# A cross network over looked-up rows: six tables instead of eight by one-hot products, and transfers in another order and queue

## The reference

```python
def _cin_layer(h0, h, W):
    Wr = W.reshape(F0, Fi, K)
    return jnp.einsum('bid,bjd,ijk->bkd', h0, h, Wr)
conv1 = _cin_layer(x, x, W1)           # 39 x 39 pairs -> 128
hidden1, final1 = conv1[:, :64, :], conv1[:, 64:, :]
conv2 = _cin_layer(x, hidden1, W2)     # 39 x 64 pairs -> 128
z = jnp.sum(jnp.concatenate([final1, conv2], axis=1), axis=2)
h = jnp.concatenate([z, dense_ctx], axis=1)
h = jnp.maximum(h @ W_top1 + b_top1, 0.0)
h = jnp.maximum(h @ W_top2 + b_top2, 0.0)
y = h @ W_top3
```

## Time and profile before

| | |
|---|---|
| median of 3 runs | 844.24 us (842.39 to 844.51) |
| profiled execution, its own time | 845.87 us |
| its span in the trace | 844.1 us |
| mean granted TensorE clock | 0.97 of full |
| busy: TensorE, VectorE, ScalarE, GpSimd | 91%, 84%, 69%, 63% |
| DMA | 180.90 MB, mean 214 GB/s |

### The profile page before, as it was taken

How to read it: one execution, slowest core, us unless ns; L and a number is a source line. 1 busy time by engine, 2 the same in 40 slices (tenths; PEclk the granted TensorE clock), 3 DMA queues, 4 the chain that set the end, 5 groups by cost and what they waited for, 6 DMA issues and landing times.

```text
span 844.1 us, 16070 instructions
## 1 busy us (share of the span) xinstructions
PE 764.4 (91%) x5816; PEld 446.9 (53%) x5816; DVE 709.4 (84%) x1176; ACT 579.6 (69%) x1547; POOL 531.1 (63%) x508
## 2 busy tenths in 40 slices
PE   1996268789999999999999999999999999999996
PEld 0563113236556656564656555655656656666666
DVE  5994469769899999888989889898989899999850
ACT  1331225748878787877687878787888888787872
POOL 6887777747777777767676767777777777400000
PEclk9998589979999999999999999999999999999999
DMA  5444988898989898989888888889898989888200
GB/s 129 141 100 130 263 208 223 245 258 237 256 238 261 232 254 233 241 226 244 232 231 235 231 243 227 254 230 253 228 251 240 255 222 281 230 263 268 77 2 1
DMA packets 137125, 180.90 MB, mean 214 GB/s; under 512 B 106587, under 2 KB 117699, under 8 KB 119061
## 3 DMA queue, kind: packets, MB, share of 16 engines
q1 hardware_dynamic: 119444, 170.27, 70.8%
q0 software_dynamic: 16128, 8.29, 6.1%
q10 hardware_dynamic: 1472, 1.30, 0.5%
HBM read 167.57 MB, written 17.21 MB: 219 GB/s over the span
## 4 chain that ended last, share of the span: by engine, by line
PE 29%; DMA 28%; DVE 24%; SPq 11%; issue 4%; ACT 2%; POOL 1%; ACTq 0%; DVEq 0%
DMA copies<-xt 25%; DVE blocks L774 21%; PE hidden L430 13%; SPq L351 9%; PE sums L457 4%; PE sums L477 4%; PE hidden L532 3%; DVE turned L796 2%; PE sums L506 2%; POOL emb L396 1%; ACT arena L631 1%; PE sums L482 1%; DMA blocks<-hot_t 1%; PE sums L494 1%; PE sums L498 1%
## 5 line engine op out<-in xcount | busy, mean ns | idle before, releaser
L396 POOL DMA_INDIRECT emb<-in_tbl,ids_tile x504 | 530.9, 1053 | 199.3 <-issue 93.2
L774 DVE TENSOR_TENSOR blocks<-copies 117x512 f32<-117x512 f32 x840 | 522.5, 690 | 91.8 <-DMA copies<-xt 51.7
L430 PE MATMUL hidden<-blocks,w_pairs 117*64 117x512 f32 x1792 | 433.9, 610 | 26.0 <-DVE blocks L774 24.0
L631 ACT ACTIVATE arena<-sums 64x480 f32<-64x480 f32 (+2 forms) x936 | 293.7, 314 | 152.0 <-PE sums L457 130.6
L430 PEld LDWEIGHTS hidden<-blocks,w_pairs 117*64 117x64 f32 x1792 | 149.5, 138 | 235.4 <-DVE blocks L774 110.0
L457 PEld LDWEIGHTS sums<-xdiag,turned 64*103 64x103 f32 x2000 | 98.2, 167 | 78.3 <-issue 34.1
L619 ACT ACTIVATE xdiag<-turned 32x468 f32<-32x468 f32 (+1 forms) x256 | 118.8, 464 | 3.1
L457 PE MATMUL sums<-xdiag,turned 64*103 64x78 f32 x2000 | 112.2, 257 | 1.8
L602 ACT ACTIVATE hid_high<-hidden 32x512 f32<-32x512 f32 x128 | 75.3, 589 | 14.0 <-PE hidden L430 12.0
L477 PE MATMUL sums<-arena,weights 128*128 128x128 f32 x640 | 82.9, 287 | 1.9 <-DVE weights L851 1.3
L477 PEld LDWEIGHTS sums<-arena,weights 128*128 128x128 f32 x640 | 77.0, 199 | 4.4 <-DVE weights L851 1.5
(11 more groups left out here) (49 smaller groups left out, 311.1 us busy)
## 6 DMA issues: line engine op xcount, KB each, us to landing
copies<-xt SPq DMA_DIRECT2D x448, 312.0 KB
emb<-in_tbl,ids_tile POOLq DMA_INDIRECT x504
xt<-emb SPq DMA_DIRECT2D x32, 152.0 KB
xt<-xt SPq DMA_DIRECT2D x16, 304.0 KB
blocks<-hot_t SPq DMA_DIRECT2D x8, 500.0 KB
xt<-emb SPq DMA_DIRECT2D x32, 104.0 KB
hot_kept_rows<-rows SPq DMA_DIRECT2D x4, 480.0 KB, 9.0
emb<-hot_kept_rows SPq DMA_DIRECT2D x15, 128.0 KB
```

What stands on the lines that cost most here:

```text
L396: pool.indirect_dma_start(out=emb[u][:, f * D:(f + 1) * D], out_offset=None, in_=tables[f], in_offset=bass.IndirectOffsetOnAxis(ap=ids_til ...
L430: mm = nc.tensor.matmul(hidden[64 * c:64 * c + 64, k % 2, bank, :], w_pairs[0:ROWS, t, bank * HALF_HID:bank * HALF_HID + HID], blocks[0:RO ...
L631: op = nc.scalar.activation(out[:, :, cols].rearrange("p h (u b) -> p h u b", u=2), g[rows, i], ACT.Copy)
L774: op = nc.vector.tensor_tensor(blocks[0:ROWS, at + c, :], a[:, cols], b[:, cols], ALU.mult)
```

## The change

Six of the 1000-row tables are looked up by products (12 lookups), so tiles 1 to 15 have 33 gathers each. The split tables move from `weights` to the buffers of copies 2 and 3, and the layers' weights are loaded in `first_tile` behind the index loads. `keep` moves from SyncE's to ScalarE's queue. In the loads of chunk 1 nothing stands between the copies, and the load of the stored rows stands before them. All products with 128 output columns are made in two halves of 64. In the tail, VectorE takes over half of the last sort, the last tile's `final_sums` waits for ScalarE's copies only before its second part, and the copy of the dense rows comes first.

```diff
-HOT = [0, 4, 10, 13, 16, 26, 28, 29]
+HOT = [0, 4, 10, 13, 16, 26]
-TABLES = 5
+TABLES = 4
...
+        tables_at = copies[0:HOT_P, 2:4, :].rearrange("p a b -> p (a b)")
-        hot_table = [weights[0:HOT_P, n % TABLES * PART_WORDS:...
+        hot_table = [tables_at[:, n % TABLES * PART_WORDS:...
...
-        FIRST_SPILLED = [5, 7, 7]
-        AT_ONCE = 24
+        FIRST_SPILLED = [5, 5, 5]
+        AT_ONCE = 36
...
                 elif chunk == 1:
                     sp.wait_ge(hot_looked, COPIES_FREE)
+                elif v in (2, 3):
+                    sp.wait_ge(hot_looked, LOOKUPS)
...
                     index(n)
...
-                    if n % 2 and n >= 7:
-                        keep((n - 7) // 2)
+                    if n == 4:
+                        sp.dma_start(weights[:, 0:N_FIN], finals).then_inc(fin_loaded, 16)
+                    if n == 5:
+                        sp.dma_start(weights[:, N_FIN:], layers).then_inc(mlp_loaded, 16)
                     spill(0, 0, [s for s in range(len(PARTS)) if FIRST_SPILLED[s] == n])
                 sp.wait_ge(spilled[0], 16 * SPILLS)
                 for v in LOAD_ORDER:
                     load_copy(0, 0, 0, v)
-                keep(KEPT - 3)
-                load_copy(0, 0, 1, 0)
-                load_copy(0, 0, 1, 1)
-                keep(KEPT - 2)
-                load_copy(0, 0, 1, 2)
-                load_copy(0, 0, 1, 3)
-                keep(KEPT - 1)
                 load_hot_rows(1)
-                load_copy(0, 0, 1, 4)
+                for v in LOAD_ORDER:
+                    load_copy(0, 0, 1, v)
                 spill(0, 1)
...
             def final_sums(tile, u, j):
                 if j == 0:
-                    pe.wait_ge(gram_out, 2 * N_GROUPS * (tile + 1))
                     if tile == TILES - 1:
+                        pe.wait_ge(gram_out, N_GROUPS * (CHUNKS - 1))
                         pe.wait_ge(gram2_out, N_GROUPS + 1)
+                    else:
+                        pe.wait_ge(gram_out, 2 * N_GROUPS * (tile + 1))
...
+                    if n == FH and tile == TILES - 1:
+                        pe.wait_ge(gram_out, 2 * N_GROUPS * (tile + 1))
                     if n < FH:
-                        mm = nc.tensor.matmul(fin_conv2, w_fin2[:, n, :], gram2[:, n, cols],
-                                              start=(n == 0), stop=(n == FH - 1))
+                        for c in range(2):
+                            part = slice(64 * c, 64 * c + 64)
+                            mm = nc.tensor.matmul(fin_conv2[part, :], w_fin2[:, n, part], gram2[:, n, cols],
+                                                  start=(n == 0), stop=(n == FH - 1))
...
             def sort_hidden(k, chunk):
-                for bank in range(BANKS):
+                for bank in range(1 if chunk == CHUNKS - 1 else BANKS):
...
+            def keep(m):
+                act.wait_ge(hot_copied, 4 * (m + 1))
+                act.dma_start(hot_kept_rows[1:TILES, :, 2 * m * D:2 * (m + 1) * D].rearrange("t p n -> p t n"),
+                              rows[:, m % 2, 1:TILES].rearrange("p t a d -> p t (a d)")).then_inc(hot_kept[m % 2], 16)
...
             for j in range(LOOKUPS):
                 stage(j)
+                if j % 4 == 1 and j > 4:
+                    keep((j - 5) // 4)
...
             copy_rows(LOOKUPS - 1)
+            keep(KEPT - 1)
...
+            def sort_last(k, chunk):
+                dve.wait_ge(hid_turned, 2 * chunk - 1)
+                dve.wait_ge(hid_pairs, pairs_done(chunk, LAST, 1))
+                for q in (1, 3):
+                    op = nc.vector.tensor_copy(hid_high[32 * q:32 * q + 32, :], hidden[32 * q - 32:32 * q, k % 2, 1, :])
+                op.then_inc(last_sorted, 1)
...
+            def dense_copy(tile):
+                at = tile % 4 * 32
+                nc.vector.tensor_scalar(z_rest[FIN1:FIN1 + DENSE, :], dense_rows[at:at + DENSE, tile // 4, :],
+                                        1.0, None, ALU.mult).then_inc(fin_out, 1)
             def final_copy(tile):
+                if tile == TILES - 1:
+                    dense_copy(tile)
...
             pair_body(PAIRS - 1, False, True)
+            sort_last(3, CHUNKS - 1)
+            turn_hidden(3, CHUNKS - 1)
             copy_gram2(CHUNKS - 2, N_GROUPS - 1)
-            turn_hidden(3, CHUNKS - 1)
```

More of the change, by code:

```diff
@@ L202, in build @@
         hid_turned = sem("hid_turned")
+        last_sorted = sem("last_sorted")
         xdiag_ready = sem("xdiag_ready")
@@ L280, in index @@
                     sp.wait_ge(ones_ready, ONES_BEFORE[n - INDICES + 1])
[L281 to L286, removed]
+                sp.dma_start(hot_index[n], hot_t[n].partition_broadcast(P)).then_inc(hot_index_loaded[n % INDICES], 16)
             def load_hot_rows(tile):
@@ L493, in layer1 @@
                 for m in range(T1 // P):
-                    mm = nc.tensor.matmul(outs1[:, m, :], wt1a[:, m * P:(m + 1) * P], z_conv2[:, :],
-                                          start=True, stop=False)
+                    for c in range(2):
+                        mm = nc.tensor.matmul(outs1[64 * c:64 * c + 64, m, :], wt1a[:, m * P + 64 * c:m * P + 64 * c + 64],
+                                              z_conv2[:, :], start=True, stop=False)
                     if m % 2 and tile < TILES - 2:
                         mm.then_inc(strides, 1)
-                    mm = nc.tensor.matmul(outs1[:, m, :], wt1b[0:FIN1 + DENSE, m * P:(m + 1) * P], z_rest[:, :],
-                                          start=False, stop=True)
+                    for c in range(2):
+                        mm = nc.tensor.matmul(outs1[64 * c:64 * c + 64, m, :],
+                                              wt1b[0:FIN1 + DENSE, m * P + 64 * c:m * P + 64 * c + 64],
+                                              z_rest[:, :], start=False, stop=True)
                 mm.then_inc(l1_done, 1)
@@ L505, in layer2 @@
                     for c in range(T1 // P):
-                        mm = nc.tensor.matmul(outs2[:, m, :], wt2[:, c, m * P:(m + 1) * P], act1[:, c, :],
-                                              start=(c == 0), stop=(c == T1 // P - 1))
+                        for half in range(2):
+                            at = m * P + 64 * half
+                            mm = nc.tensor.matmul(outs2[64 * half:64 * half + 64, m, :], wt2[:, c, at:at + 64], act1[:, c, :],
+                                                  start=(c == 0), stop=(c == T1 // P - 1))
                         if c == 1 and tile < TILES - 2:
@@ L514, in layer3 @@
                 for c in range(T2 // P):
-                    mm = nc.tensor.matmul(misc[:, 0:1], act2[:, c, :], wt3[:, c:c + 1],
-                                          start=(c == 0), stop=(c == T2 // P - 1))
+                    for half in range(2):
+                        part = slice(64 * half, 64 * half + 64)
+                        mm = nc.tensor.matmul(misc[part, 0:1], act2[:, c, part], wt3[:, c:c + 1],
+                                              start=(c == 0), stop=(c == T2 // P - 1))
                 mm.then_inc(y_done, 1)
@@ L605, in sort_hidden @@
                 act.wait_ge(hid_sorted, 2 * chunk + 1)
+                if chunk == CHUNKS - 1:
+                    act.wait_ge(hid_pairs, pairs_done(chunk, LAST, BANKS - 1))
                 for q in (1, 3):
@@ L788, in relu @@
                 op.then_inc(ready, 1)
+            def sort_last(k, chunk):
[4 more added lines that the diff above has]
+                op.then_inc(last_sorted, 1)
             def turn_hidden(k, chunk):
+                if chunk == CHUNKS - 1:
+                    dve.wait_ge(last_sorted, 1)
                 for high in (1, 0):
@@ L803, in final_copy @@
                 nc.vector.tensor_scalar(z_conv2[:, :], fin_conv2, 1.0, None, ALU.mult).then_inc(fin_out, 1)
-                at = tile % 4 * 32
-                nc.vector.tensor_scalar(z_rest[FIN1:FIN1 + DENSE, :], dense_rows[at:at + DENSE, tile // 4, :],
-                                        1.0, None, ALU.mult).then_inc(fin_out, 1)
+                if tile < TILES - 1:
+                    dense_copy(tile)
             def y_copy(tile):
```

17 lines of the change are left out of this document (6 added, 11 removed).

## The result

The changed kernel takes 811.4 us (median of 4 runs, 808.5 to 818.4) against 843.3 (median of 4, 835.9 to 844.5) for the kernel before on the same chip: a ratio of 0.965, 95% interval 0.957 to 0.974. The forecast was 821.5 with a range of 810 to 832. The profiled execution took 808.5, its span is 806.6. Some executions of one kernel come out more than 1.5% above its fastest without any change of the code; the medians, ranges and ratios here leave these slow runs out.

A forecast was written before the change was run, and what follows sets the result against it. No engine bounds the whole; TensorE, DMA and VectorE are nearly equal loop limits, GpSimd a fourth. Tile 2's `turn_x` at 171.7, three tiles at 43.5, ten taking 442.6 plus 0.7, and a 76.0 tail gave 821.5 us, range 810 to 832.

The forecast's parts named there:

- The mark of tile 2: Start of tile 2's `turn_x`, forecast at 171.7 against 192.0 before, from gathers ending at 153.9 and its spill at 155.
- Tile 0's gathers: Front: with twelve lookups, the last five or six gathers gain about 1 us; tile 1's first gather starts at 66.9.
- ScalarE's and VectorE's holes: Front: ScalarE's 26.84 us wait and VectorE's waits of 9.14 and 7.04 us go; tile 1's `turn_x` at 125, not 140.7.
- Tile 1's spill: Tile 1's 33 gathers end at 110.4; the last spill follows about 1 us later, near 111.5, before at 123.96.
- GpSimd's 43.5 us a tile: Loop: 33 gathers need 43.5 us of GpSimd a tile, setting the pace of three tiles, up to tile 5 at 302.2.
- Rival 3: Gathers slowed as beside comparisons: at 1.39 us or more each the kernel is slower than before; 860 at 1.42; chance 0.03.
- The ten late tiles: Loop from tile 5 on: ten tiles take the 442.6 us of before plus 0.7 for the gathers' DMA, ending at 745.5.
- rival 1: Late copies vanish, their DMA backlog having begun with tile 1's weights; all tiles run at 43.5, end 813; chance 0.17.
- The weights: Layers' weights leave tile 1's DMA time, where they cost 11 us, for 24 to 35 us, where DMA is 0.40 filled.
- Products of 64 columns: Halved products take 208 against 222 ns: 0.5 us of TensorE a tile, nothing in the loop, 0.5 in the tail.
- Rival 4: Halved products do not overlap, each pass costing 111 ns: 8.4 us more a tile, end near 950; chance 0.02.
- Tail: After the last `turn_x`: 3.0 us less than 79.0, bounds 1.5 to 5, including 1.7 from the last `final_sums` starting earlier.

The follow-up runs named there:

- b_two: Kernel before with only COPIES_FREE changed, so one-hot operands go round two places from the fifth lookup on, not the ninth: 826.4 us against 831.0, ratio 0.996.
- b_keep_act: Kernel before with `keep` moved to ScalarE's queue and chunk 1's copies in usual order behind `load_hot_rows(1)`: 836.8 us against 835.3, ratio 1.003.
- a_eight: Changed kernel with the eight product tables of before, 31 gathers a tile, `keep` still on ScalarE's queue: 822.7 us, 0.988 of the kernel before.
- a_wide: Changed kernel with the products of 128 columns whole again: 808.1 us; run again beside the unedited changed kernel, 806.9 against 807.3.
- a_four: Changed kernel with four tables looked up by products, 35 gathers a tile: 839.7 us, 1.011 of the kernel before.
- b_index128: Kernel before with only the index loads going to 128 partitions instead of 125: 835.3 and 829.1 us (2 runs) against 835.3.
- a_weights_late: Changed kernel with the layers' weights loaded in tile 1 again, as before: 816.4 us.
- a_tail_old: Changed kernel with the tail's order as before, its products still in halves: 812.0 us, with a tail of 77.7 us.

## Why the prediction was right, and where its terms were off

The range held, but 811.4 lies below the 815 to 827 that the forecast itself named, and the gain is 31.9 us where 22.7 were forecast. The mark of tile 2 was forecast at 171.7 and came at 171.68; the loop took 561.4 in place of 573.8, the tail 73.5 in place of 76.0. These 12.4 and 2.5 us are all the distance from 821.5 to the span of 806.6.

**Tile 0's gathers, a mis-sized term.** "The last five or six gain about 1 us": the spill moved by 8.5. I had priced a gather beside comparisons at 1.42 us, the step from 66.54 to 67.96, where the comparisons are parted; from the first gather to the fortieth the mean step was 1.67, with five long ones in it. How long a gather takes depends on how long the comparisons run unbroken, and fewer places for operands break the runs; `b_two` shows it alone. The Trainium skill (SBUF — State Buffer, Who interferes with whom) says that a VectorE instruction in a two-port mode locks GpSimd out, so that it can't write descriptors, while VectorE instructions with two inputs from SBUF contend only with a GpSimd operation that reads SBUF. The traces fit both, though they don't show in which mode L837 ran: 3.59 us beside L837, 0.94 beside L774 in the loop; but most gathers beside L837 took 1.1 to 1.3, and those that stood did so over several instructions, to the end of the pair.

**ScalarE's and VectorE's holes** vanished as written: `b_keep_act` has neither of them. It adds what I had missed: after the move alone `load_hot_rows` waits in SyncE's queue, unless the last store is issued ahead of the copy loads. From VectorE's first multiplication to `turn_x` of tile 1 the forecast gave 42 us, and the trace 42.7.

**Tile 1's spill, a wait that the forecast had wrong.** It gave 1.1 us from the end of the last gather to the last spill. That gather, the 72nd of all, started at 100.24 and was over at 101.18, 9 us earlier than forecast, and the spill left only at 109.81. It did not wait for the gather. SyncE's queue, with the 28 copy loads of tile 0 just issued, stood for 14.86 us at one issue of tile 1's first spill, and the last spill then waited for the first one to land, since it copies rows that the first has written:

```profile
89.05 14.86 SPq L320 DMA_DIRECT2D xt<-emb  x1
```

```profile
SPq L315 <- DMA xt<-emb: 1.1, 1, 1.1
```

**The mark of tile 2, right by luck.** Its sum was 153.9 for the end of tile 2's gathers, 1.1 to the spill and 16.7 from there to `turn_x`. The gathers ended at 144.07, the spill left at 149.67 and `turn_x` came 22.0 later: two errors of 5.3 us that cancel. The 16.7 is no fixed delay: `turn_x` comes behind VectorE's multiplications of the tile before and reads nothing that the spill writes, and the step was 16.7 and 22.8 for tiles 1 and 2 before, 8.2 and 22.0 after. Within tile 1 (118.0 to 171.7) VectorE waited 10.1 us for copies, with the DMA 0.89 busy: so a front that led the forecast by 7 us at tile 1 led by nothing at tile 2. In the repeat of the same kernel the mark came at 167.0.

**GpSimd's 43.5 us a tile as the pace of the next three, a path that was wrong.** Its rows give 32.34 busy + 33 x 0.30 = 42.2, and the three tiles took 42.4. But `a_eight` has tiles of 42.4 too, with 31 gathers: TensorE sets them, busy for 41.82 of 42.40. That it could run below 43.1 I had counted as nothing. SyncE does wait for gathers in the loop (7 times and 11.5 us between 230 and 700 us), as forecast, but `a_wide` with 6 such waits and 10.6 us there has no late tile: they are not what sets the pace. Rival 3's slowing did not appear, and `a_four` puts the margin at less than two gathers.

**The ten late tiles.** I kept the 442.6 of before plus 0.7; they took 434.1. The step that failed is to treat a backlog as a property of the kernel. It varies from execution to execution, and perhaps with the chip: `b_two` and `b_index128`, with the same loop as before, had 43.2 and 43.5 a tile from tile 3 on, `a_wide` none above 43.2. In time rival 1 was nearly right (813), but its cause is not: the changed kernel loads no weights in tile 1 and still has tiles of 44.5 to 46.5, and the kernels that load them there had late tiles in some traces only. In a slow tile of after (516.69 to 563.21, 46.5 us), the chain before it reads:

```profile
489.99 6.32 DMA emb<-in_tbl,ids_tile
496.32 0.54 SPq L316
...
497.62 6.80 DMA xt<-emb
504.43 0.73 SPq L350
...
512.15 12.72 DMA copies<-xt
```

The gather's rows land 6.32 us after its start, the spill waits, the copies wait for the spill and then take 12.72 us. In this tile late gathers and late copies are one chain, but a late tile needs no late gather: in the tile of `a_eight` from 261.5, 45.1 us long, copies took 13.24 us with no wait for a gather in the chain. What starts it in one tile and not in the next stays open.

**The weights.** Forecast 11 us, which the sum did not use as a term; `a_weights_late` puts them at 9 to 10, and 5 of these are in tile 2 itself, so the price holds.

**Products of 64 columns.** In the loop no gain, as forecast: 807.3 against 806.9 for the whole kernel. In the tail 1.9 (75.4 to 73.5), where I had 0.5; 1.2 of it lie ahead of the last `final_sums`. The loads of L477 and L473 up to the next L430 and L420, before and after:

```profile
716.08 0.20 PEld L430 LDWEIGHTS hidden<-blocks,w_pairs 117*64 117x64 f32 x4
```

```profile
682.25 2.16 PEld L473 LDWEIGHTS sums<-arena,weights 128*64 128x64 f32 x40
684.38 0.37 PEld L518 LDWEIGHTS sums<-weights,act 128*64 128x64 f32 x8
684.66 0.20 PEld L420 LDWEIGHTS hidden<-blocks,w_pairs 117*64 117x64 f32 x4
```

2.41 us from the first load to L420's, against 716.08 - 713.31 = 2.77 before, 0.36 less. The pass prices of the forecast give 24 x (111 - 104) ns = 0.17. The other 0.19 may be the change of tiling mode, which halves leave out before L420; no run separates it. Rival 4 did not occur.

**Tail, mis-sized.** Forecast 3.0, bounds 1.5 to 5; measured 5.5. `final_sums` starts right behind L518, as written, 58.3 us after the last `turn_x` in place of 61.3, and its 80 passes run at full clock:

```profile
791.22 0.40 PE L518 MATMUL sums<-weights,act 128*64 128x1 f32 x8 [0.71 <-DVE act L800]
791.47 4.57 PE L473 MATMUL sums<-arena,weights 128*64 128x128 f32 x80
```

They take 4.57 us in place of 6.36: 1.8, for which I had taken 0.5 by the clock and a part of the halves' 0.5. Two more kernels part the two, the old order with halves (`a_tail_old`) and the new one with whole products (`a_wide`):

```profile
793.98 6.25 PE L469 MATMUL sums<-arena,weights 128*64 128x128 f32 x80 [0.87 <-ACT arena L630]
```

```profile
786.71 4.71 PE L471 MATMUL sums<-arena,weights 128*128 128x128 f32 x40
```

Halves alone save 0.11 to 0.14 us, the order 1.65 to 1.68: the old order's passes meet the half clock, the new order's don't. The rest of the 5.5 is the earlier start (3.0, forecast 1.7) and 0.7 behind `final_sums`.

## What to carry to other kernels

Read the long single instructions of an engine beside what ran at that moment, before pricing it by a row from a quiet place: 8.5 us lay in a few gathers that stood behind an unbroken run of comparisons. A wait that is removed from one queue is to be followed to the next that needs the same store, as here from ScalarE to SyncE. A time between two marks is a term of a sum only if the second waits for the first; here 16.7 us stood for a step that measured 8.2 to 22.8. And where engines stand within 2% of each other, a saving on one (0.7 us a tile of TensorE) may bring nothing; measure it alone beside the whole before counting it, and don't take the waits that appear beside it for the cause before a kernel without them has been looked at.

## What the runs showed that I had not expected

- In each of the five unbroken pairs of comparison runs of the kernel before, one gather stood till the pair ended (2.07 to 4.68 us in place of 1.2); in `b_two`, where 0.12 to 0.21 us parted the runs, none did.
- With 28 copy loads issued ahead of it, one DMA issue of SyncE took 14.86 us in place of 0.6, and a spill whose gathers were done left 8.6 us after the last of them.
- From a gather's start to its rows' landing it took 2.24 us at the end of tile 0, and 6.32 in the loop with copy loads in the DMA.
- One reordering of the tail kept TensorE's granted clock at 1.00 where it was 0.50, 1.7 us in `final_sums` alone.
- The kernel before differed by up to 13 us between chips (830.1 to 843.3).
